# Gathers issued only when the fifth in front has landed, on five rotating semaphores

## What is computed

```python
theta = x[dst] - x[src]
w = sigmoid(relu(theta @ W1 + b1) @ W2 + b2)
agg = segment_sum(w * theta, dst, num_segments=n_nodes)
indeg = segment_sum(ones((dst.shape[0], 1)), dst, num_segments=n_nodes)
gnn = agg + indeg * (x @ W4 + b4)
out = layernorm(x + gnn)
```

## Time and profile before

| | us |
|---|---|
| median of 3 runs | 4755.34 |
| lowest and highest | 4750.17, 4755.39 |
| the profiled execution | 4802.18 |
| its span, first to last instruction | 4800.4 |
| POOL, DVE busy in it | 3054.6, 2931.3 |
| PE, ACT busy in it | 1967.7, 1241.4 |

### The profile page before, as it was taken

One profiled execution on the slowest core, in us unless ns is written; L12 is line 12 of the kernel. 1 busy time (PEld: TensorE's weight loads), 2 busy tenths in 40 slices (PEclk: granted clock), 3 DMA queues, 4 the chain that ended last, 5 costly groups with the idle time before them and its releaser, 6 DMA issues.

```text
span 4800.4 us, 43092 instructions
## 1 busy us (share of the span) xinstructions
PE 1967.7 (41%) x10791; PEld 1814.8 (38%) x10791; DVE 2931.3 (61%) x4882; ACT 1241.4 (26%) x2277; POOL 3054.6 (64%) x3229
## 2 busy tenths in 40 slices
PE   2134444443434444444443444444434444444434
PEld 2133334433333334433343434334334344333333
DVE  2046566666656666666665666666666666666666
ACT  0122222222222222222222222222222222222222
POOL 6666666666666666666666666666666666666665
PEclk6556666656666666566666665666666666666665
DMA  5544545554544545444555555545554554455453
GB/s 174 144 130 145 144 144 145 147 144 145 146 144 146 152 137 152 145 146 146 145 146 143 147 145 151 146 143 144 147 146 145 145 145 146 145 147 149 142 149 103
DMA packets 347031, 695.14 MB, mean 145 GB/s; under 512 B 128517, under 2 KB 216875, under 8 KB 346527
## 3 DMA queue, kind: packets, MB, share of 16 engines
q0 software_dynamic: 152240, 412.56, 31.2%
q10 hardware_dynamic: 44965, 214.31, 13.5%
q1 hardware_dynamic: 149578, 65.51, 5.2%
HBM read 666.86 MB, written 31.64 MB: 146 GB/s over the span
## 4 chain that ended last, share of the span: by engine, by line
DVE 52%; another core or an unknown queue 28%; issue 15%; PE 4%; DVEq 1%; DMA 0%; ACT 0%; SPq 0%; ACTq 0%
DVE diff L738 10%; DVE ps_z L732 10%; DVE scaled_x L761 9%; DVE logit L746 8%; DVE hot_en L751 5%; PE ps_sum L595 2%; DVE square L714 2%; DVE rstd L716 1%; DVE mix L795 1%; DVE y L797 1%; PE ps_z L578 1%; DVE stats L800 1%; DVE own L772 1%; DVE sums L767 1%
## 5 line engine op out<-in xcount | busy, mean ns | idle before, releaser
L567 POOL DMA_INDIRECT arena<-table,src_at x3069 | 2903.6, 946 | 1646.5 <-issue 890.1
L595 PE MATMUL ps_sum<-scaled_x,hot_en 128*128 128x130 f32 x6446 | 1400.1, 401 | 1764.8 <-DVE scaled_x L761 1100.9
L595 PEld LDWEIGHTS ps_sum<-scaled_x,hot_en 128*128 128x128 f32 x6446 | 1309.7, 307 | 1837.6 <-issue 1837.6
L732 DVE TENSOR_TENSOR ps_z<-ps_z,arena 128x896 f32<-128x896 f32 x439 | 480.9, 1095 | 1400.9 <-remote 1212.1
L659 ACT ACTIVATE ps_log<-logit,b_col 128x7 f32<-128x7 f32 x461 | 124.5, 270 | 3191.7 <-DVE logit L746 2032.7
L746 DVE TENSOR_REDUCE logit<-diff 128x7 f32<-128x896 f32 x461 | 499.4, 1083 | 37.1 <-issue 1.4
L738 DVE SCALAR_TENSOR_TENSOR diff<-ps_z,w_rows 128x896 f32<-128x896 f32 x461 | 502.6, 1090 | 15.8
L751 DVE TENSOR_TENSOR hot_en<-ps_win,rel 128x896 f32<-128x896 f32 x461 | 497.9, 1080 | 0.0
L652 ACT ACTIVATE hot_ne<-away,ones_col 126x896 bf16<-126x896 bf16 x461 | 479.8, 1041 | 43.3 <-issue 1.1
L644 ACT ACTIVATE away<-dst_rows,neg_ids 126x896 bf16<-126x896 int32 x461 | 473.9, 1028 | 2.6 <-issue 2.6
L761 DVE TENSOR_TENSOR scaled_x<-arena,ps_log 128x896 f32<-128x896 f32 x439 | 473.3, 1078 | 0.0
(11 more groups left out here) (87 smaller groups left out, 931.6 us busy)
## 6 DMA issues: line engine op xcount, KB each, us to landing
dst_rows<-in_dst ACTq DMA_DIRECT2D x230, 882.0 KB
arena<-table,src_at POOLq DMA_INDIRECT x3069
parts<-parts_of SPq DMA_DIRECT2D x461, 31.5 KB
parts_of<-stage SPq DMA_DIRECT2D x115, 96.0 KB
winT<-in_x_cols SPq DMA_DIRECT2D x115, 64.0 KB
window<-in_x SPq DMA_DIRECT2D x115, 64.0 KB
out<-yout SPq DMA_DIRECT2D x115, 64.0 KB
arena<-in_x_turned SPq DMA_DIRECT2D x25, 250.0 KB
```

The lines of the kernel that those rows point to most:

```text
L567: nc.gpsimd.indirect_dma_start(gath[:, slot_of(g) + t, :], None, table, ids)\
L595: last = nc.tensor.matmul(ps_sum[:, 0:SW], hot_en[:, b, t, :], scaled_x[:, b, t, :], start=(g == 0 and t == 0), stop=(stop and t == tiles_ ...
L732: v.tensor_tensor(ps_z[b][:, 0:n, :], ps_z[b][:, 0:n, :], u, ALU.subtract).then_inc(z_read, 1)
```

## The change

A constant `AHEAD = 5` comes in. Gathers are numbered, the held ones and the ringed ones each from 0 on, `m`. Gather m adds to semaphore m % 5. From m = 5 on, POOL waits before gather m until that semaphore has reached the value that gather m-5 gives it, and adds 1 to `pool_gate`. So no more than five gathers of a kind are issued and not yet landed. The waits for `scaled` and `z_ready` stay as they are. A reader no longer waits on one semaphore but on all five, for the last five gathers of what it needs (`wait_landed` in DVE's `difference`, and the loop in PE's `turn_held`). Buffers, gathers, their order and their sizes don't change.

```diff
--- before.py
+++ after.py
@@ -27,6 +27,9 @@
 NEAR = 42
 WK = 3 * NEAR
 SW = F + 2
+
+
+AHEAD = 5
 
 
 RB = 6
@@ -260,13 +263,13 @@
         parts_out = sems("parts_out", 2)
         parts_in = sems("parts_in", 2 * NB)
         rows_of_dst_in = sems("rows_of_dst_in", 2)
-        held_in = sem("held_in")
+        held_in = sems("held_in", AHEAD)
         heldT_ready = sem("heldT_ready")
         heldT_copied = sem("heldT_copied")
         held_u_ready = sem("held_u_ready")
         held_u_copied = sem("held_u_copied")
         x_copied = sem("x_copied")
-        gathered = sems("gathered", RB)
+        gathered = sems("gathered", AHEAD)
         away_ready = sem("away_ready")
         hot_ready = sem("hot_ready")
         z_ready = sem("z_ready")
@@ -337,8 +340,15 @@
         def slot_of(g):
             return (place[g] % RB) * BT
 
-        def landed(g):
-            return 16 * (BT * (place[g] // RB) + tiles_of(g))
+
+
+        def first_of(g):
+            return place[g] * BT
+
+        def wait_landed(eng, g):
+            end = first_of(g) + tiles_of(g)
+            for m in range(end - AHEAD, end):
+                eng.wait_ge(gathered[m % AHEAD], 16 * (m // AHEAD + 1))
 
 
 
@@ -432,7 +442,8 @@
 
 
         def turn_held(pe, h, q):
-            pe.wait_ge(held_in, 16 * BT * HELD)
+            for m in range(HELD * BT - AHEAD, HELD * BT):
+                pe.wait_ge(held_in[m % AHEAD], 16 * (m // AHEAD + 1))
             wait(pe, held_u_copied, h * PAIRS + q)
             for t, e in enumerate(pair(q)):
                 last = nc.tensor.transpose(ps_hid[:, t * P:(t + 1) * P], held_x[:, h * BT + e, :], ident[:, :])
@@ -550,8 +561,12 @@
                     pool.wait_ge(turned, PACE[h])
                     pool.sem_inc(pool_gate, 1)
                 for t in range(BT):
+                    m = h * BT + t
+                    if m >= AHEAD:
+                        pool.wait_ge(held_in[m % AHEAD], 16 * (m // AHEAD))
+                        pool.sem_inc(pool_gate, 1)
                     ids = bass.IndirectOffsetOnAxis(ap=src_at[:, g * BT + t:g * BT + t + 1], axis=0)
-                    nc.gpsimd.indirect_dma_start(held_x[:, h * BT + t, :], None, x, ids).then_inc(held_in, 16)
+                    nc.gpsimd.indirect_dma_start(held_x[:, m, :], None, x, ids).then_inc(held_in[m % AHEAD], 16)
             wait_for_table(pool)
             pool.wait_ge(judged, 1)
             pool.sem_inc(pool_gate, 1)
@@ -563,9 +578,13 @@
                     pool.wait_ge(z_ready, ringed[n - 3] + 1)
                     pool.sem_inc(pool_gate, 1)
                 for t in range(tiles_of(g)):
+                    m = first_of(g) + t
+                    if m >= AHEAD:
+                        pool.wait_ge(gathered[m % AHEAD], 16 * (m // AHEAD))
+                        pool.sem_inc(pool_gate, 1)
                     ids = bass.IndirectOffsetOnAxis(ap=src_at[:, g * BT + t:g * BT + t + 1], axis=0)
                     nc.gpsimd.indirect_dma_start(gath[:, slot_of(g) + t, :], None, table, ids)\
-                        .then_inc(gathered[place[g] % RB], 16)
+                        .then_inc(gathered[m % AHEAD], 16)
 
 
         def windows_tensor(pe):
@@ -727,7 +746,7 @@
                     dve.wait_ge(held_u_copied, (held_no[g] + 1) * PAIRS)
                     u = held_u[:, 0:n, :]
                 else:
-                    dve.wait_ge(gathered[place[g] % RB], landed(g))
+                    wait_landed(dve, g)
                     u = gath[:, slot_of(g):slot_of(g) + n, 0:F]
                 v.tensor_tensor(ps_z[b][:, 0:n, :], ps_z[b][:, 0:n, :], u, ALU.subtract).then_inc(z_read, 1)
                 dve.wait_ge(z_read, g + 1)
```

## The result

| | us |
|---|---|
| before, median of 4 runs | 4755.12 (4750.17 to 4755.39) |
| the change, median of 4 runs beside them | 4804.86 (4804.07 to 4805.54) |
| ratio, with its 95% interval | 1.0102 (1.009 to 1.0114) |
| profiled execution of the change, its span | 4804.70, 4802.9 |

The change is 1.0% slower. The range of 4500 to 4870 holds the time because it was wide enough to take in the case "somewhat slower" (0.20); the forecast itself, no change within 0.2%, missed by 48 us.

A forecast was written before the change was run, and what follows sets the result against it. Bound taken: 1.4 us per gather plus a 0.7 us restart per 14, through PE's late announcements. 4802.2 + 2 + 0 + 0 + 0 + 0 = 4804, scaled to 4757 us in the median; range 4500 to 4870.

The forecast's parts named there:

- somewhat slower: Outcome case for the whole kernel: 4765 to 4870 us, chance 0.20.
- What bounds the kernel: Gather loop: z_ready announced about 1.4 us per gather after a run began, plus 0.7 us restart per 14 gathers.
- full relief: Faster rival, POOL's stops all gone: 4088 us, 4048 in the median; half or all gone had chance 0.13.
- The sum itself: Profiled 4802.2 us plus 2 and zeros gives 4804, scaled by 4755.3 / 4802.2 to 4757 us in the median.
- (1): POOL's wait for the fifth gather in front: landing may take 5.55 us, takes 2.95; cost 0 to 2 us.
- My sign for (1) being wrong: Gaps appearing inside a run of POOL's gathers beside the dst_rows loads.
- my slower rival: Landings over 5.55 us bind and announcements count from the last gather: up to 4951 us in the median; slower 0.30.
- (2): POOL's 3213 added waits and pool_gate increments: 0 us, hidden in the 0.95 us of the gather in front.
- (3): DVE's 439 and PE's 88 waits on five counters come behind the wait for z_ready: 0 us.
- (4): Head, first held gathers: slower landings may make them wait, POOL's 5.56 us stand takes it up; 0 to +2 us.
- (5): Limit of five doesn't lift the hold on PE's announcement, as it exists with three out: 0 us.
- the signs I named: Remote waits near 600 us in 180, no landing wait listed, DVE about 1360 us remote, 3.4 us stop after 14.

The follow-up runs named there:

- the paced kernel: The kernel before with a 128x128 memset on POOL ahead of each ringed gather, second set: 4829.5 us, ratio 1.004.
- the earlier trace: The trace the prediction read: kernel before, unchanged, profiled execution 4802.2 us, span 4800.4; none of the four runs of before.
- The third set: Last four experiment kernels (waits doubled, change again, change without increments, 256-wide memset) against the kernel before at 4066.4 us; chip 0 by the record.
- the first set: Before again, held part alone, ringed part alone, limit of eight, beside the result's runs; kernel before at 4755 us, chip 13.
- the second set: Never-binding waits on POOL, added waits on DVE, POOL paced, limit of three, against the kernel before at 4805.7 us, chip 0.

## Why the prediction was right, and where not

**What bounds the kernel: right, but only for two of three sets.** About 1.4 us per gather from the start of a run, with the announcement of z held meanwhile, is what the paced kernel confirms, and the trace's own records of updates bear out the reading: in the earlier trace rows PE's last matmul for z ends at 2403.28 us and its update stands at 2414.72. The third set goes at POOL's 1.25 us, without any hold. The price that I gave for full relief was right to 0.5%, though nothing in this change brought it about. The sum itself took the trace for an exception of 1.0% and scaled it to 4755.3; it was the ordinary time of another set.

**(1) Waits that bind: mis-sized.** I read a landing twice, 2.95 and 2.83 us, both in the first 20 us of the loop and neither beside a load of dst_rows (the whole trace has a median of 2.45 us from a gather's start to its last packet, and 4.51 at the 90th percentile), and a restart of 0.70 us from the start of DVE to that of POOL, which is not the restart from a landing. Measured in the third set: 1.41 us of restart or more, landings of 4.70 us at the 90th percentile. In the first set this was mostly covered as I said: 45.4 us in 72 waits appear (24 net), and with eight allowed none holds POOL while the time stays. My sign for (1) being wrong, waits inside runs, did appear, but it is not what the 1.0% are made of. Where the cover is gone, the same waits cost 229 of the 251 us by which the trace is longer. That was my slower rival's other condition, though in a form I hadn't thought of: I asked whether the stop is counted from the last gather, when it could be absent. The rival's time, "somewhat slower", came true in the first set without its cause; that the range held the result is luck to that extent.

**(2) The instructions: the step that failed.** I set 0 us, hidden in the 0.95 us of the gather in front, with 32 us as the upper bound. That the gap stays at 0.30 us was right. But the pitch wasn't the thing that bounds the loop; the 1.4 us per gather were, and by my own account these were not the engine's. Waits that never bind, each with its increment, cost 73 us in the second set, and twice as many cost nothing in the third, where the pitch bounds. Both costs, 47 us for the ringed part in the first set and 73 in the second, are over my upper bound of 32. The cost goes with the hold. That the 41 to 49 us in the loop of the first set are this same cost is what the runs suggest: the run of 14 gathers grows there by 0.16 us (20.49 to 20.65), in the second set by 0.20, and neither DVE's waits nor, with eight allowed, landings are left to explain it. It was not shown in that set by a run of its own, and the rotating semaphores were never tried by themselves. Nor was the instruction parted from its semaphore update where there is a hold: the kernel without increments, which does this, met the third set alone.

**(3) DVE's waits: right.** 0.06%, with an interval that holds zero. PE's 88 waits at turn_held were not tried by themselves.

**(4) The head: mis-sized.** I took 0 to 2 us and held that POOL's stop for `PACE` before 171.03 takes up delays. The held gathers after the change:

```profile
14.54 0.95 POOL L569 DMA_INDIRECT held_x<-in_x,src_at  x1 [4.53 <-DMA held_x<-in_x,src_at]
...
34.68 0.94 POOL L569 DMA_INDIRECT held_x<-in_x,src_at  x1 [5.43 <-DMA held_x<-in_x,src_at]
...
176.31 0.94 POOL L569 DMA_INDIRECT held_x<-in_x,src_at  x1 [5.55 <-PE ps_z L428]
...
198.40 0.94 POOL L569 DMA_INDIRECT held_x<-in_x,src_at  x1 [2.66 <-DMA held_x<-in_x,src_at]
```

The early waits (4.53, 5.43 us) do go into the wait for the table. But the last stop for it now ends at 176.31 rather than 171.03, and a landing costs 2.66 us even behind it, at 198.40; the first ringed gather starts at 233.4 in place of 222.2. Not all of these 11 us are the limit's: in the six traces of the first two sets in which the held gathers have no limit, the first ringed gather starts anywhere from 219.7 to 228.7 us. By the medians the held part alone costs 7 us in the first set. In the third the start differs by 1.4 us (209.6 against 208.2).

**(5) No relief: right for five.** The stop stays at 3.3 us, the waits on "remote" are 576.0 us in 174, and DVE's are 1311.3 in 181: the signs I named, but for the one that no wait on a landing would be listed. With three allowed POOL's remote waits all but vanish, yet PE's updates still come late, and more is paid for the landings than is gained.

## What to carry to other kernels

An instruction that hides behind its own engine's work was free here where that engine's pitch set the pace, and not where something else did; first find out what sets it. A limit on transfers in flight must be costed with the slow landings, those beside the largest load, and with the restart from a landing, not with the typical ones. And before two traces are compared, make sure that each agrees with its medians, and run the kernel before anew beside every set of experiments: a trace that is 1% longer than the medians is a warning, and the chip's number alone didn't tell the sets apart.

## What the runs showed of the hardware

The same kernel takes 4755, 4806 and 4066 us in three sets of runs, the last two on chips with the same number. In the first two sets PE's results reach DVE and POOL late, 11 us in the run of 14 gathers of the earlier trace rows and 22 us in the earlier trace rows, at a rate of some 1.4 us per gather; in the third at once. It is above all PE's updates that are late: in the trace the median is 3.23 us for z_ready, and 0.01 us for the updates of DVE, ACT and POOL. The granted clock is 0.628 to 0.642 in the runs of the kernel before in the first two sets and 0.654 to 0.661 in the third, where PE has the same work in less time; nothing shows it to be the cause. What occupies those 1.4 us, and why the third set doesn't have it, the runs leave open. One suspicion wasn't tested, that the recording itself has to do with it. The executions of the experiments have each a span and a granted clock of their own and so were being recorded, those of the medians too, and the hold goes with missing records of semaphore updates. An added increment on POOL makes one more update (73 us in 3064 of them), the added waits on DVE make none (no difference). Whether the hold exists without recording, these runs can't say.

On POOL's side, a gather never started sooner after the last packet that it waited for than 1.06 us (three allowed), 1.08 (five, without increments) and 1.41 (five, in the third set), and mostly about 2 us.
